# Cross attention of a decoder layer: a list of its own for the first batch's preparation, part of it moved behind the first scores

## What is computed

```python
q = x @ Wq.T + bq                       # x: layer norm of (4, 512, 256)
kv = c @ Wkv.T + bkv                    # c: (4, 1601, 256)
k, v = kv[..., 0], kv[..., 1]           # after the split in 16 heads of 16
q = _rms_norm(q, q_gamma)               # over the 16 numbers of each head
k = _rms_norm(k, k_gamma)
scores = jnp.einsum('bhnd,bhmd->bhnm', q, k) * scale
attn = jax.nn.softmax(scores, axis=-1)
out = jnp.einsum('bhnm,bhmd->bhnd', attn, v)
```

## Time and profile before

| | |
|---|---|
| median of 3 runs | 1317.8 us (1315.87 to 1321.56) |
| the profiled execution | 1319.82 us, its span 1318.1 us |
| mean granted TensorE clock in it | 0.989 of full speed |
| busy share of the span | TensorE 92%, ScalarE 69%, POOL 54%, VectorE 50% |

### The profile page before, as it was taken

How to read it: one execution, slowest core, us unless ns; L and a number is a source line. 1 busy time by engine, 2 the same in 40 slices (tenths; PEclk the granted TensorE clock), 3 DMA queues, 4 the chain that set the end, 5 groups by cost and what they waited for, 6 DMA issues and landing times.

```text
span 1318.1 us, 27754 instructions
## 1 busy us (share of the span) xinstructions
PE 1209.0 (92%) x8712; PEld 739.7 (56%) x8712; DVE 659.2 (50%) x2198; ACT 907.4 (69%) x1824; POOL 706.0 (54%) x810
## 2 busy tenths in 40 slices
PE   5999999999999885799999999999999989999897
PEld 4667766776677573433334333433333278888794
DVE  6666567557655556555035502552555163333336
ACT  4656556646645615667986798679998848888892
POOL 1776557656756701445415540564267757765552
PEclk9999999999999998899999999999999999999999
DMA  7998665445445721001001100101056386666677
GB/s 236 361 318 274 240 206 189 170 153 188 172 149 192 239 64 35 26 13 31 17 1 51 33 17 2 51 2 35 29 208 227 115 302 197 200 219 195 193 270 301
DMA packets 146756, 195.05 MB, mean 148 GB/s; under 512 B 12049, under 2 KB 132513, under 8 KB 145969
## 3 DMA queue, kind: packets, MB, share of 16 engines
q1 hardware_dynamic: 135856, 162.97, 37.9%
q0 software_dynamic: 10752, 30.26, 6.2%
HBM read 71.01 MB, written 122.18 MB: 147 GB/s over the span
## 4 chain that ended last, share of the span: by engine, by line
PE 55%; ACT 16%; issue 10%; DVE 8%; DMA 5%; POOL 3%; SPq 2%; ACTq 0%; DVEq 0%; POOLq 0%
ACT xa_probs L1404 9%; PE sa_pf L354 8%; PE xa_banks L1243 7%; PE xa_banks L1258 6%; PE sa_po L436 5%; PE xa_banks L1126 5%; PE sa_pf L387 4%; PE sa_ps L411 4%; PE mo_banks L2172 4%; PE sa_ptr L422 4%; DMA mo_xs<-rows 3%; ACT sa_probs L478 2%; PE mo_banks L2181 2%; DMA mo_w_all<-in_down_p 1%; PE mo_banks L2160 1%
## 5 line engine op out<-in xcount | busy, mean ns | idle before, releaser
L1404 ACT ACTIVATE xa_probs<-xa_banks 128x1024 f32<-128x1024 f32 (+1 forms) x416 | 401.9, 1045 | 83.2 <-PE xa_banks L1243 82.3
L341 POOL TENSOR_SCALAR sa_probs<-sa_probs,sa_recip 128x128 f32<-128x128 f32 (+3 forms) x256 | 275.7, 1090 | 170.1 <-DVE sa_recip L598 169.6
L478 ACT ACTIVATE sa_probs<-sa_probs,sa_neg_max 128x128 f32<-128x128 f32 (+3 forms) x256 | 141.8, 555 | 155.4 <-DVE sa_neg_max L535 155.3
L1258 PE MATMUL xa_banks<-xa_probs,xa_v_one 128*17 128x512 f32 (+1 forms) x1664 | 218.7, 598 | 6.9 <-ACT xa_q_aug L1350 4.6
L1243 PE MATMUL xa_banks<-xa_q_aug,xa_k_aug 32*128 32x512 f32 (+1 forms) x1664 | 153.3, 442 | 13.5 <-issue 3.4
L2088 POOL DMA_INDIRECT slots<-mo_y,mo_dest x128 | 123.9, 968 | 69.5 <-issue 35.5
L2172 PE MATMUL mo_banks<-mo_xs_t,mo_gu 128*128 128x128 f32 x1024 | 136.3, 276 | 0.0
L2172 PEld LDWEIGHTS mo_banks<-mo_xs_t,mo_gu 128*128 128x128 f32 x1024 | 125.5, 193 | 0.4 <-issue 0.2
L535 DVE CUSTOM_DVE_ANT_0 sa_probs<-sa_ps,sa_toeplitz 128x128 f32<-128x128 f32 (+3 forms) x256 | 115.1, 486 | 14.9 <-PE sa_ps L411 13.4
L1243 PEld LDWEIGHTS xa_banks<-xa_q_aug,xa_k_aug 32*128 32x128 f32 (+1 forms) x1664 | 61.5, 179 | 106.2 <-ACT xa_probs L1404 74.5
L2232 ACT ACTIVATE mo_gu<-mo_w_all 128x512 f32 x128 | 80.7, 630 | 35.3 <-issue 15.3
(11 more groups left out here) (343 smaller groups left out, 2287.5 us busy)
## 6 DMA issues: line engine op xcount, KB each, us to landing
rows<-sa_blank SPq DMA_DIRECT2D x128, 548.0 KB, 3.8
mo_xs<-rows SPq DMA_DIRECT2D x106, 137.0 KB
slots<-sa_blank SPq DMA_DIRECT2D x48, 256.0 KB, 5.0
mo_w_all<-slots SPq DMA_DIRECT2D x22, 512.0 KB, 16.5
xa_raw<-in_ctx_t SPq DMA_DIRECT2D x24, 256.0 KB, 2.8
mo_w_all<-in_gate_up_p SPq DMA_DIRECT2D x2, 2816.0 KB, 16.1
sa_toeplitz<-extended_bias SPq DMA_DIRECT2D x8, 512.0 KB, 7.6
mo_w_all<-in_down_p SPq DMA_DIRECT2D x2, 2048.0 KB, 16.9
```

The costliest lines, as they stand in the source:

```text
L341: pool.tensor_scalar(probs[:, t % SLOTS, 0:w], probs[:, t % SLOTS, 0:w], recip[:, col:col + 1], None, ALU.mult).then_inc(probs_ready, 1)
L478: act.activation(probs[:, t % SLOTS, 0:w], probs[:, t % SLOTS, 0:w], ACT.Exp, bias=neg_max[:, i:i + 1], scale=-1.0, accum_out=sums[:, i:i ...
L1258: last = pe.matmul(banks[32 * i:32 * i + XD + 1, 6 + group % 2, :], v_one[b % 2][0:m, c, 4 * g + i, :], probs[0:m, (2 * j + i // 2) % RING ...
L1404: act.activation(probs[0:m, n % RING, :, :], banks[0:m, 2 * (n % 3):2 * (n % 3) + 2, :], ACT.Exp).then_inc(probs_ready, 1)
```

## The change

The preparation of batch 0 gets a list of its own, FIRST, of 29 steps. TensorE branches after 25 of them (BRANCH_AT). Its other nine steps, kt 8 to 12 and qt 4 to 7 (BEHIND), go into slots 2 to 10 of batch 0's attention. Batch 0's slots 11 to 51 then hold all 38 steps for batch 1, in the order of PLAN (the table moved gives slot for slot; each helper's place goes with it through slot_in). Batches 1 to 3 keep their places.

The steps' helpers are put in tables by (b, s). In batch -1 the key splits now go to POOL (norms_k and splits side by side), the marks k0_hi_done and the key parts of high_first and low_first are gone, and cuts of the context come earlier in the list. A group's squares wait for the sum of the group before (sq_summed), no longer for its rms. The query norm is in slots 15 to 18 of FIRST.

The wait for the whole preparation ahead of each batch is replaced by waits in scores on the fills that are needed. The nine late fills are copied out by VectorE, and so are the transposes in five slots (CHANGES), the last ones ahead of a change of banks. One of the five, batch 0's slot 27, now holds a kv, which VectorE copies in any case. The x norm, before one call at slot 44, is made in five parts: batch 1's at slots 6 to 10 of batch 0, batch 2's at 47 to 51; batch 3's five parts stay together at slot 44. VectorE's branch ahead of batch 0 moves to the end of slot 10.

```diff
-    RMS_AT = [4, 16, 23, 26]
-    NORM_K_AT = [7, 8, 9, 10, 19, 20, 21, 22, 26, 27, 28, 29, 30]
-    SPLIT_AFTER = 3
+    FIRST = [("kv", 0), ("kv", 1), ("kv", 2), ("kv", 3), ("x", 0), ("x", 1), ("kv", 4), ("kv", 5),
+             ("q", 0), ("q", 1), ("kv", 6), ("kv", 7), ("kt", 0), ("kt", 1), ("kt", 2), ("kt", 3),
+             ("kv", 8), ("kv", 9), ("kv", 10), ("kv", 11), ("kt", 4), ("kt", 5), ("kv", 12), ("kt", 6),
+             ("kt", 7), ("qt", 0), ("qt", 1), ("qt", 2), ("qt", 3)]
+    BRANCH_AT = 25
+    BEHIND_AT = 2
+    BEHIND = [("kt", 8), ("kt", 9), ("kt", 10), ("kt", 11), ("kt", 12), ("qt", 4), ("qt", 5), ("qt", 6), ("qt", 7)]
+    BEHIND_END = BEHIND_AT + len(BEHIND)
+    O_AT = 4
+    O_SLOTS = [O_AT + KT * i for i in range(QUADS)]
     CUTS = -(-KT // 2)
-    CUT_AT = {4: 2, 6: 3, 12: 4, 17: 5, 21: 6}
-    CUT_NEXT_AT = {31: 0, 33: 1}
-    SQUARE_Q_AT = 10
-    RMS_Q_AT = 11
-    NORM_Q_AT = 14
-    GAIN_Q_AT = 15
-    CUT_Q_AT = [16, 29]
-    LOAD_AT = {5: 4, 7: 5, 13: 6}
-    LOAD_NEXT_AT = {18: 0, 22: 1, 32: 2, 34: 3}
-    LOAD_X_AT = 15
+    CHANGES = [(0, 27), (0, 40), (1, 27), (1, 40), (2, 27)]
     STORE_AT = 6
-    NORM_X_AT = 44
-    O_AT = 4
-    PRO_BANKS = [6, 7, 0, 1, 2, 3, 4, 5]
...
+    behind_slots = [s for s in range(BEHIND_END, SLOTS) if s not in O_SLOTS]
+    moved = dict(zip(real, behind_slots))
+
+    def slot_in(b, s):
+        if b != 0:
+            return s
+        later = [moved[r] for r in real if r >= s]
+        return later[0] if later else SLOTS - 1
+
+    steps = {}
+    for s, step in enumerate(FIRST):
+        steps[-1, s] = step + (0,)
+    for n, step in enumerate(BEHIND):
+        steps[0, BEHIND_AT + n] = step + (0,)
+    for b in range(B - 1):
+        for s in real:
+            steps[b, moved[s] if b == 0 else s] = PLAN[s] + (b + 1,)
+    for b in range(B + 1):
+        for s in O_SLOTS:
+            if s in slots_of(b) and b * SLOTS + s > KT:
+                steps[b, s] = ("o", (b * SLOTS + s) // KT - 1, None)
+    steps.update(ROUTE)
 
     def step_of(b, s):
-        if (b, s) in ROUTE:
-            return ROUTE[b, s]
-        step = PLAN[s]
-        if step is None or step[0] == "o" and not (b >= 0 and b * SLOTS + s > KT):
-            return None
-        if step[0] != "o" and b + 1 >= B:
-            return None
-        return step
+        return steps.get((b, s))
+
+    loads, x_loads, cuts, squares_q, cuts_q = {}, {}, {}, {}, {}
+    rms_parts, norms_k, splits, q_parts, q_norms, q_gains, x_norms = {}, {}, {}, {}, {}, {}, {}
+
+    def put(table, b, s, what):
+        table.setdefault((b, s), []).append(what)
+
+    for s, g in ((5, 4), (8, 5), (12, 6)):
+        put(loads, -1, s, (0, g))
+    for s, g in ((1, 2), (6, 3), (10, 4), (15, 5), (19, 6)):
+        put(cuts, -1, s, (0, g))
+    for g, at in enumerate(((3, 4, 5), (12, 13, 14), (26, 27, 28))):
+        for part, s in enumerate(at):
+            put(rms_parts, -1, s, (0, g, part))
+    for part in range(3):
+        put(rms_parts, 0, part, (0, 3, part))
+        put(q_parts, -1, 15 + part, (0, part))
+    put(squares_q, -1, 9, 0)
+    put(q_norms, -1, 18, 0)
+    put(q_gains, -1, 18, 0)
+    put(cuts_q, -1, 20, (0, 0))
+    put(cuts_q, 0, 5, (0, 1))
+    for c in range(KT):
+        put(norms_k, -1 if c < 8 else 0, c + 8 if c < 8 else c - 8, (0, c))
+        put(splits, -1 if c < 8 else 0, c + 8 if c < 8 else c - 8, (0, c))
+    put(loads, -1, 18, (1, 0))
+    put(loads, -1, 22, (1, 1))
+    put(x_loads, -1, 24, 1)
+    put(loads, 0, 7, (1, 2))
+    put(loads, 0, 8, (1, 3))
+    put(cuts, 0, 6, (1, 0))
+    put(cuts, 0, 7, (1, 1))
+    for part in range(5):
+        put(x_norms, 0, 6 + part, (1, part))
+    for b in range(B - 1):
+        nb = b + 1
+        for s, g in ((5, 4), (7, 5), (13, 6)):
+            put(loads, b, slot_in(b, s), (nb, g))
+        for s, g in ((4, 2), (6, 3), (12, 4), (17, 5), (21, 6)):
+            put(cuts, b, slot_in(b, s), (nb, g))
+        for g, at in enumerate((4, 16, 23, 26)):
+            for part in range(3):
+                put(rms_parts, b, slot_in(b, at) + part, (nb, g, part))
+        for c, s in enumerate((7, 8, 9, 10, 19, 20, 21, 22, 26, 27, 28, 29, 30)):
+            put(norms_k, b, slot_in(b, s), (nb, c))
+        for c in range(KT):
+            put(splits, b, slot_in(b, PLAN.index(("kt", c)) - 3), (nb, c))
+        put(squares_q, b, slot_in(b, 10), nb)
+        for part in range(3):
+            put(q_parts, b, slot_in(b, 11) + part, (nb, part))
+        put(q_norms, b, slot_in(b, 14), nb)
+        put(q_gains, b, slot_in(b, 15), nb)
+        put(cuts_q, b, slot_in(b, 16), (nb, 0))
+        put(cuts_q, b, slot_in(b, 29), (nb, 1))
+        if nb + 1 < B:
+            for s, g in ((18, 0), (22, 1), (32, 2), (34, 3)):
+                put(loads, b, slot_in(b, s), (nb + 1, g))
+            put(x_loads, b, slot_in(b, 15), nb + 1)
+            for s, g in ((31, 0), (33, 1)):
+                put(cuts, b, slot_in(b, s), (nb + 1, g))
+            for part in range(5):
+                put(x_norms, b, 47 + part if b == 0 else 44, (nb + 1, part))
+
+    def by_scalar(b, s):
+        kind, _, batch = step_of(b, s)
+        if b < 0:
+            return kind in ("kt", "qt", "x", "kv")
+        return kind in ("kt", "qt") and batch > 0 and (b, s) not in CHANGES
...
-                    pool.wait_ge(rms_ready, batch * 4 + g)
+                    pool.wait_ge(sq_summed, batch * 4 + g)
...
+                if b == 0 and j < 2:
+                    wait_out(pe, max(first_held[bank] for bank in ((0, 1, 2, 3), (4, 5))[j]))
+                if b == 0 and g == 0:
+                    wait_out(pe, fill_of(b, "kt", c))
+                elif j % SLOTS == 0:
+                    wait_out(pe, fill_of(b, "kt", KT - 1))
+                if c == 0 and (b == 0 or g == 2):
+                    wait_out(pe, fill_of(b, "qt", 2 * g + 1))
...
-            run(-1, False)
+            for s in range(BRANCH_AT):
+                prepare(-1, s)
             pe.wait_ge(const_ready, 3)
             pe.wait_ge(gain_done, 1)
             risk = pe.value_load(unsafe[0:1, 0:1], min_val=0, max_val=1)
             with pe.If(risk > 0):
+                for s in range(BRANCH_AT, len(FIRST)):
+                    prepare(-1, s)
+                for s in range(BEHIND_END):
+                    prepare(0, s)
                 for b in range(B):
                     wait_out(pe, prepared[b])
                     largest(b)
                     run(b, True)
             with pe.Else():
+                for s in range(BRANCH_AT, len(FIRST)):
+                    prepare(-1, s)
                 for b in range(B):
-                    wait_out(pe, prepared[b])
                     run(b, False)
...
-            def rms_part(part, squares, total, out, tmp, done):
+            def rms_part(part, squares, total, out, tmp, done, summed=None):
                 if part == 0:
-                    chain.then_wait(dve.tensor_reduce(total, squares, AX.X, ALU.add))
+                    last = dve.tensor_reduce(total, squares, AX.X, ALU.add)
+                    if summed is None:
+                        chain.then_wait(last)
+                    else:
+                        last.then_inc(sq_summed, 1)
+                        dve.wait_ge(sq_summed, summed)
...
-            def normalise_x(batch):
-                dve.wait_ge(x_norm_in, 16 * (batch + 1))
-                layernorm(dve, chain, xn, xn, TT, stats, mean_var, var[:], rstd[:], tmp[:]
-                          ).then_inc(xn_ready, 1)
+            def normalise_x(batch, part):
+                if part == 0:
+                    dve.wait_ge(x_norm_in, 16 * (batch + 1))
+                    for t in range(TT):
+                        last = dve.bn_stats(stats[:, t, :], xn[:, t, :])
+                    chain.then_wait(last)
+                elif part == 1:
+                    for t in range(TT):
+                        last = dve.bn_aggr(mean_var[:, t, :], stats[:, t, :])
+                    chain.then_wait(last)
+                    chain.then_wait(dve.tensor_scalar(var[:], mean_var[:, 0:TT, 1], LN_EPS, None, ALU.add))
+                    chain.then_wait(dve.tensor_scalar(rstd[:].bitcast(I32), var[:].bitcast(I32), -0.5,
+                                                      float(RSQRT_MAGIC), ALU.mult, ALU.add))
+                    newton(rstd[:], var[:], tmp[:])
+                elif part == 2:
+                    newton(rstd[:], var[:], tmp[:])
+                    newton(rstd[:], var[:], tmp[:])
+                else:
+                    for t in range(2 * (part - 3), 2 * (part - 2)):
+                        last = dve.tensor_scalar(xn[:, t, :], xn[:, t, :], mean_var[:, t, 0:1], rstd[:, t:t + 1],
+                                                 ALU.subtract, ALU.mult)
+                    if part == 4:
+                        last.then_inc(xn_ready, 1)
```

(28 more changed lines are left out.)

172 lines of the change are left out of this document (73 added, 99 removed).

## The result

Before: 1317.7 us (1315.3 to 1321.6, 7 runs). After: 1308.1 us (1301.0 to 1310.1, 7 runs). The ratio is 0.9918, 95% interval [0.9895, 0.9941]: 9.6 us gained where 14.6 were forecast. The profiled execution of the changed kernel took 1309.5 us, its span is 1307.4, 10.7 shorter than the one of before.

What follows compares the result with a forecast made beforehand. The prediction took a chain across engines in batch 0's preparation, not one engine, as the bound. Its terms, -14.6 + 1.5 - 1.5 = -14.6 us, took the median from 1317.8 to 1303.2 us; range 1297 to 1309.

Steps and rivals of the forecast that it cites:

- the first rival: Batch 0's preparation: POOL costs VectorE little and the branch's 3.4 us hides under a copy; 1297 to 1299 us, chance 0.2.
- the second's: Second rival, batch 0's slots 2 to 7: late key splits and queries hold TensorE, 5 us lost, 1308 us; chance 0.17.
- The sum -14.6: Whole kernel: first exponential 14.6 us earlier, batch 0 1.5 longer, changes of banks 1.5 gained.
- kv 12 at 518 to 519: Sign in batch 0's preparation: when its last keys and values start, 517.58 us before the change.
- walk through the new order: Batch 0's preparation followed: kv 12 starts at 514.3 us, first exponential at 523.1, before POOL's cost.
- 4.5 for POOL: Batch 0's preparation: POOL's new splits slow VectorE and delay the first exponential by 4.5 us; bounds nothing to 8.2.
- kv 12 to first exponential, 8.9: End of batch 0's preparation: kv 12, transposes, branch and first scores take 8.9 us, 24.6 before.
- The branch's gap of 3.4: TensorE's stand at its branch, expected between key and query transposes and counted as 3.4 us.
- Batch 0, +1.5: Batch 0's 52 slots, with fills in slots 2 to 10, take 134.1 us against 132.65: 1.5 lost.
- The handover rival: Batch 0's slots 2 to 7: late key splits and queries hold TensorE, 5 us lost, 1308 us; chance 0.17.
- Changes of banks, -1.5: Slots 28 and 41: VectorE's copies cut 2.77 to 2.29 us; three such slots outside batch 0 gain 1.5.
- all of POOL's splits wholly in the chain: Batch 0's preparation: with POOL's 14.4 us of splits the chain stays as long, nothing measurable, 1312 to 1319 us; chance 0.08.

Runs made afterwards that it cites:

- the second profile: The changed kernel run again unaltered, beside the other follow-up kernels: 1307.8 us.
- c1_busy_loads: Changed kernel plus 30 extra 512-column matmuls on TensorE ahead of kv 12, and context cuts 2 and 3 loaded ahead of the last store: 1309.7 us.
- u3_changes_back: Changed kernel with the five copies at changes of banks given back to ScalarE: 1307.8 us.
- u2_all_ahead: Changed kernel with the nine late fills put ahead of the first scores again and batch 0's slots 2 to 10 empty: 1316.4 us.
- u4_old_order: Changed kernel with the 29 fills ahead in the old list's order, nine still behind and splits still on POOL: 1307.8 us.
- b1_branch22: Changed kernel with context cuts 2 and 3 loaded ahead of the last store and TensorE's branch moved ahead of kv 12: 1301.7 us.
- the early loads: Changed kernel with context cuts 2 and 3 loaded ahead of the self attention's last store: 1303.7 us, and 1303.0 us when repeated.

## Why the prediction was right, and where its size was off

The direction, the mechanism and the range (1297 to 1309) held, the range only just: 1308.1 is near its upper end and outside the 1301 to 1306 of the forecast. The range was said to run from the first rival's middle to the second's; by their own numbers that is 1298 to 1308. The sum -14.6 came out as -10.7 in the profile: first exponential -11.3, batch 0 +2.5, batches 1 and 2 -1.5, the rest -0.4.

- **kv 12 at 518 to 519**: 518.29, right, but by luck, with two errors that mostly cancel. The prediction's walk through the new order gave 34.7 us from kv 0, and 4.5 for POOL. Measured are 38.2, and 36.6 without the late load. So what POOL took is 1.9 together with the walk's other errors. The queries' ten steps alone took 5.1 (508.19 to 513.64 without the key add's 0.35) in place of 2.55, beside 4.78 of POOL: 0.53 per us where 0.7 was taken. The key adds (0.42) and the reduction (1.21) beside POOL were untouched, as assumed. By the Trainium skill's rule (SBUF — State Buffer, Who interferes with whom), taken one for one, it would have been 4.78 (an estimate); the trace shows 2.55. "The loads of SP are asked for in the same order; none was among the long waits" failed: cut 2 is needed earlier now, and its load was queued behind the last store, which costs 1.6 us.
- **kv 12 to first exponential, 8.9**: this is the term that was mis-sized, 12.6 and 10.2 measured. It used durations at full clock for kv 12, key and query transposes (1.4 + 1.0 + 1.8 = 4.2). At half clock they took 2.6 + 1.9 + 3.6 = 8.1. That and the gap of 3.35 are nearly all of the 12.6; it was 10.2 in the second profile, where the branch's gap was 1.76. With TensorE kept at full clock it was 9.1 (c1_busy_loads), near the 8.9. I had put TensorE's wait into the walk (it grows from 2.81 to 7.89) without asking what its clock does behind it.
- **The branch's gap of 3.4**, now between key and query transposes: 3.35, right. Taken as unavoidable; moved into the wait it is hidden.
- **Batch 0, +1.5**: +2.5. Slots 0 and 1 took 4.3 in place of 3.7. The slots 2 to 10 were 2.04 to 2.64 but for one of 3.33, which overlaps with 3.4 us of half clock at 534.1; together 21.4 in place of 20.2. The rest came out 0.8 under its sum. Nothing was late: kt 8's split ended at 527.5 and was read at 537.0, and TensorE waited for no split up to 553. The handover rival, at 1308 the nearest in its number, was wrong in its cause.
- **Changes of banks, -1.5**: -1.0 and -0.5 in batches 1 and 2, right in size; u3_changes_back gives 1.6 back in the trace. Too small for the medians. But slots 28 and 41 did not fall to 2.29: they are 2.59 and 2.51 in batch 1 (2.77 and 2.89 before), and the other half of the gain is in the slots ahead of them, 27 and 40 (2.03 and 2.08 for 2.29 and 2.28). In batch 2 only slot 27's copy had moved, so slot 41 could not fall and stayed at 3.13.
- **Where the gain comes from**: the walk had all of it behind kv 12 (24.6 down to 8.9, that is 15.7) and a loss of 1.2 ahead (kv 12 at 514.3 + 4.5 for 517.58). Measured are 12.0 to 14.4 behind and a loss of 0.3 to 0.4 ahead. u2_all_ahead shows that the nine moved fills carry nearly all of it, and u4_old_order that the order of the others does not matter. The rival "all of POOL's splits wholly in the chain" was wrong: taken off POOL they cost 1.9 more.

The Trainium skill (Runtime: NRT & Kernel Launch, Instruction fetch mechanics) says that a taken branch whose target lies outside the pages held on the chip stalls until the target's page is fetched. The traces agree, with the fetch and the 1.6 us behind it; and in b1_branch22 the fetch stands at 508.67 to 510.89, inside the wait.

Still open: why the medians gain 4 to 5 from the early loads, where the chain to kv 12 gains 1.6 (the spans differ by 3.3 to 5.8). A part lies far behind: from the last exponential to the end the profiles with the early loads took 266.4 and 267.7 us, those of the changed kernel 268.1 and 270.8; that the loads are the cause is not shown. Open too is what lets the fetch of the branch start, since the end of the key transposes doesn't: in nine of the ten profiles with the gap it begins 3.6 to 3.9 us after kv 12 does, at either clock.

## What to carry to other kernels

Behind a long wait of TensorE count its next work at half clock for the upper end of the range, and put whatever it must do without data, such as a branch, into that wait. Then leave filler matmuls out: the branch uses the wait up. When a fill moves earlier, follow its load too, past the stores queued ahead of it on its queue. When a small edit slows a far part of the kernel, compare the time to landing of each load and look for an instruction fetch in the middle of it before you form a theory of the edit's own effect.
